# Weight chunks of experts 5 to 8 moved from the attention steps to between the routed jobs

## The reference

```
# attention: 4 sequences of 512 tokens, width 512; q and k come from ctx (width 128)
qp = ctx @ Wq.T + bq ;  kp = ctx @ Wk.T            (+ bk)
scores = qp @ kp.T * 128**-0.5 * layernorm(x)
x = x + softmax(where(mask, -inf, scores))
# feed-forward on xn = layernorm(x): one shared expert and the best 2 of 8
shared = silu(xn @ shared_gate_w) * (xn @ shared_up_w) @ shared_down_w
top_val, top_idx = top_k(xn @ router_w, 2) ;  p = sigmoid(top_val)
for each expert e: g, u = split((p_e * xn) @ gate_up_w[e]) ;  y_e = (silu(g) * u) @ down_w[e]
out = x + shared + sum of y_e over the two chosen experts
```

## Time and profile before

| | |
|---|---|
| median of 3 runs | 365.19 us (364.84 to 365.95) |
| the profiled execution | 365.61 us, its span 363.9 us |
| TensorE busy | 320.0 us (88%) |
| VectorE, ACT, GpSimd busy | 208.1, 177.6, 231.0 us |
| attention steps | from about 14 to 126 us |
| tables | about 126 to 162 us |
| routed jobs | about 162 us to the end |
| on ACT: exponential, and its sum read out | 0.73 and 0.19 us |
| two copies of x (L506, L507), two projections (L483) | 0.59 each; 1.25 the pair |
| high copy of a chunk (L493), copy of ctxT (L478), rw_hi (L538) | 1.04; 0.58; 0.23 us |
| idle of GpSimd before the scatters, for landings of earlier ones | 47.9 us in 21 waits |

### The profile page before, as it was taken

The page is one execution under the profiler, slowest core; times in us unless marked ns, Lnnn a source line. Parts: engine busy times, 40 slices in busy tenths (PEclk is TensorE's granted clock), DMA queues, the critical chain, the costliest instruction groups (busy, mean ns, idle before and its releaser), DMA issues.

```text
span 363.9 us, 6490 instructions
## 1 busy us (share of the span) xinstructions
PE 320.0 (88%) x1627; PEld 217.8 (60%) x1627; DVE 208.1 (57%) x461; ACT 177.6 (49%) x400; POOL 231.0 (63%) x199
## 2 busy tenths in 40 slices
PE   2857999899999994648999999999999999999991
PEld 1324666576666762315776766777777777777760
DVE  0666887898998889612444444444444444444440
ACT  2467767667757645102644434444444444444430
POOL 0688999886675739948376565656555465555433
PEclk9999999999999998556999999999999999999998
DMA  7956788746646420075346466857666666575736
GB/s 186 304 203 200 222 241 239 272 145 214 221 146 196 153 86 0 0 193 165 57 92 98 83 116 118 143 95 125 113 113 117 115 119 116 91 130 86 134 36 82
DMA packets 29763, 50.61 MB, mean 139 GB/s; under 512 B 5472, under 2 KB 9312, under 8 KB 29728
## 3 DMA queue, kind: packets, MB, share of 16 engines
q0 software_dynamic: 9008, 21.66, 33.7%
q1 hardware_dynamic: 19232, 27.99, 24.3%
q10 hardware_dynamic: 1488, 0.54, 0.7%
HBM read 30.45 MB, written 19.73 MB: 138 GB/s over the span
## 4 chain that ended last, share of the span: by engine, by line
PE 48%; POOL 19%; issue 10%; ACT 7%; DMA 7%; DVE 6%; POOLq 0%; SPq 0%; DVEq 0%; ACTq 0%
PE bank L948 9%; PE bank L958 8%; PE bank L953 8%; POOL gu_lo L356 7%; PE bank L981 5%; PE bank L987 5%; PE bank L984 5%; POOL dn_lo L356 5%; PE bank L1072 4%; DMA out_rows<-y,jscatter 3%; POOL rstd L332 3%; PE bank L967 2%; ACT gu_hi L493 2%; ACT bank L488 2%; POOL pen L351 2%
## 5 line engine op out<-in xcount | busy, mean ns | idle before, releaser
L439 POOL DMA_INDIRECT out_rows<-y,jscatter x39 | 61.9, 1588 | 73.5 <-DMA out_rows<-y,jscatter 47.9
L958 PE MATMUL bank<-gu_hi,x_lo 128*128 (+1 forms) x220 | 70.9, 444 | 0.0
L948 PE MATMUL bank<-gu_hi,x_hi 128*128 (+1 forms) x220 | 62.4, 406 | 3.4 <-POOL dn_lo L356 1.4
L953 PE MATMUL bank<-gu_lo,x_bf 128*128 (+1 forms) x220 | 57.5, 384 | 0.0
L670 DVE TENSOR_TENSOR x_lo<-bank,x_hi 128x512 fp32r<-128x512 f32 x55 | 37.7, 686 | 26.4 <-ACT x_bf L507 25.3
L863 DVE SCALAR_TENSOR_TENSOR h<-bank,xg,h 128x256 f32<-128x256 f32 x39 | 18.9, 484 | 58.4 <-ACT h L594 57.0
L420 POOL DMA_INDIRECT xg<-xn_rows,jgather x39 | 41.7, 1069 | 16.1 <-issue 15.1
L514 ACT CAST h_hi<-bank 128x256 fp32r<-128x256 f32 x55 | 20.6, 374 | 60.9 <-PE bank L967 59.0
L958 PEld LDWEIGHTS bank<-gu_hi,x_lo 128*128 128x128 f32 x220 | 42.0, 191 | 12.7 <-issue 0.3
L356 POOL TENSOR_TENSOR gu_lo<-stage,gu_hi 128x1024 bf16<-128x1024 f32 x18 | 43.4, 2412 | 9.7 <-ACT gu_hi L493 9.7
L948 PEld LDWEIGHTS bank<-gu_hi,x_hi 128*128 128x128 f32 x220 | 40.5, 190 | 13.7 <-issue 3.1
(11 more groups left out here) (128 smaller groups left out, 491.5 us busy)
## 6 DMA issues: line engine op xcount, KB each, us to landing
stage<-in_L_ffn_gate_up_w SPq DMA_DIRECT2D x16, 512.0 KB, 3.8
xin<-in_x SPq DMA_DIRECT2D x16, 256.0 KB, 4.3
xn_rows<-xn SPq DMA_DIRECT2D x16, 256.0 KB, 3.8
stage<-in_L_ffn_down_w SPq DMA_DIRECT2D x8, 512.0 KB, 3.8
out_rows<-x SPq DMA_DIRECT2D x16, 256.0 KB, 4.2
out_rows<-zeros POOLq DMA_DIRECT2D x1, 1024.0 KB, 5.0
ctx_in<-in_ctx SPq DMA_DIRECT2D x1, 768.0 KB, 8.8
xg<-xn_rows,jgather POOLq DMA_INDIRECT x39
```

Of the source, the lines that this page charges most:

```text
L439: g.indirect_dma_start(out=out, out_offset=bass.IndirectOffsetOnAxis(ap=jscatter[:, n - TILES:n - TILES + 1], axis=0), in_=y[:, r, :], in_ ...
L948: tn.matmul(ps_g(n)[:], x_hi[:, n % TS, k, :], gu_hi[:, e, k, :], start=(k == 0), stop=False)
L953: tn.matmul(ps_g(n)[:], x_bf[:, n % TS, k, :], gu_lo[:, e, k, :], start=False, stop=False)
L958: last = tn.matmul(ps_g(n)[:], x_lo[:, n % TS, k, :], gu_hi[:, e, k, :], start=False, stop=(k == KC - 1))
```

## The change

It lets `EARLY` be 15: each of the steps 3 to 14 converts one chunk, step 0 two, step 1 one, step 2 none. In the steps from 2 on the low part stands ahead of pair_inv_std, in the steps 0 and 1 behind it. Chunk 15 comes at the end of the attention, 16 to 18 behind the first gathers, and the other eight (19 to 26) in the jobs: their high copies in the jobs 2, 4, ... 16, their low parts behind the scatters of the jobs 3, 5, ... 17. CAREFUL becomes 20. In the first steps the order of projections, transposes, statistics and conversions is changed on all four engines, TensorE gets 8 + 14 transposes of the identity that nobody reads (keep_busy), and rw_hi and rw_lo move to step 1.

```diff
-EARLY = 3 * (E - 1)
+EARLY = 15
-CAREFUL = 8
+CAREFUL = 20
+SPREAD = CHUNKS - EARLY - 4
...
         def chunks(s):
-            return range(2 * s, 2 * s + 2) if s < 6 else range(s + 6, s + 7) if s < TILES - 1 else range(0)
+            if s == 0:
+                return range(0, 2)
+            return range(2, 3) if s == 1 else range(s, s + 1) if 3 <= s < TILES - 1 else range(0)
...  # GpSimd
             penalty(1)
-            first_inv_std(1)
             g.memset(zeros[:], 0.0).then_inc(zero_s, 1)
             pool.wait_ge(zero_s, 1)
             g.dma_start(out_t[TILES:TILES + XS].rearrange("r p d -> p r d"),
                         zeros[:].unsqueeze(1).to_broadcast([P, XS, D])).then_inc(st_trash, 16)
+            first_inv_std(1)
...
-                if i < 2:
+                if place >= 7 and i < 2:
...
-                else:
+                elif place >= 7:
                     pool.wait_ge(max_s, TILES)
                 low_part(c)
...
-                for c in chunks(s)[0:1]:
-                    low_part(c)
-                pair_inv_std(s)
-                for c in chunks(s)[1:]:
-                    low_part(c)
+                if s < LAG:
+                    pair_inv_std(s)
+                if s == 0:
+                    low_part(0)
+                elif s == 1:
+                    low_part(1)
+                    low_part(2)
+                else:
+                    for c in chunks(s):
+                        low_part(c)
+                    pair_inv_std(s)
...
                 scatter(n)
-                if n in (TILES + 1, TILES + 2):
-                    late_low(READY + 3 + n - TILES - 1)
+                if TILES + 3 <= n < TILES + 2 * SPREAD + 3 and (n - TILES) % 2:
+                    late_low(READY + 3 + (n - TILES - 3) // 2)
...  # ACT
             ctx_copy(1)
-            act.wait_ge(ld_rw, 16)
-            a.copy(rw_hi[:], rw[:]).then_inc(rwhi_s, 1)
...
                 expo(s)
-                if s + 1 < B:
-                    projections(s + 1)
-                if s + 2 < B:
-                    ctx_copy(s + 2)
+                if s == 0:
+                    projections(1)
+                    high_part(0)
+                    ctx_copy(2)
+                if s == 1:
+                    x_high(0)
+                    high_part(1)
+                    projections(2)
+                    high_part(2)
+                    ctx_copy(3)
+                    act.wait_ge(ld_rw, 16)
+                    a.copy(rw_hi[:], rw[:]).then_inc(rwhi_s, 1)
+                if s == 2:
+                    projections(3)
                 if j >= 0:
                     half_tanh(j)
-                for c in chunks(s):
-                    high_part(c)
-                if s >= 1:
+                if s >= 2:
+                    for c in chunks(s):
+                        high_part(c)
                     x_high(s - 1)
...
-                if n in (TILES + 1, TILES + 2):
-                    late_high(EARLY + 4 + n - TILES - 1)
+                if TILES + 2 <= n < TILES + 2 * SPREAD + 2 and (n - TILES) % 2 == 0:
+                    late_high(EARLY + 4 + (n - TILES - 2) // 2)
...  # VectorE
+            v.tensor_scalar(kpad_pen[:], kpad_in[:], MASKED, None, ALU.mult).then_inc(pen_ready, 1)
             x_stats(0)
             x_mean(0)
-            v.tensor_scalar(kpad_pen[:], kpad_in[:], MASKED, None, ALU.mult).then_inc(pen_ready, 1)
-            x_stats(1)
-            x_mean(1)
-            dve.wait_ge(rwhi_s, 1)
-            v.tensor_tensor(rw_lo[:], rw[:], rw_hi[:].bitcast(f32), ALU.subtract).then_inc(rwlo_s, 1)
             for s in range(TILES):
...
                 neg_max(s)
+                if s == 0:
+                    x_stats(1)
+                    x_mean(1)
...
                         x_low(s - 1)
+                    if s == 1:
+                        dve.wait_ge(rwhi_s, 1)
+                        v.tensor_tensor(rw_lo[:], rw[:], rw_hi[:].bitcast(f32), ALU.subtract).then_inc(rwlo_s, 1)
...  # TensorE
+            def keep_busy(count):
+                for _ in range(count):
+                    tn.transpose(bank[2][:, 0:P], ident[:], ident[:])
+
             pe.wait_ge(c_ident, 1)
+            keep_busy(8)
...
             last.then_inc(wT_ps, 1)
+            keep_busy(14)
             ctx_transpose(0)
             projections(0)
+            scores(0)
+            scores(1)
             ctx_transpose(1)
-            scores(0)
+            projections(1)
+            ctx_transpose(2)
...
-                if s + 1 < B:
-                    projections(s + 1)
-                if s + 2 < B:
-                    ctx_transpose(s + 2)
+                if s == 0:
+                    projections(2)
+                    ctx_transpose(3)
                 if j == 0:
+                    pe.wait_ge(lo_s, 2)
+                if j == 1:
                     pe.wait_ge(lo_s, 3)
...
-                if s + 1 < TILES:
+                if 1 <= s < TILES - 1:
                     scores(s + 1)
+                if s == 1:
+                    projections(3)
```

More of the change, by code:

```diff
@@ L536, in _ @@
             ctx_copy(1)
-            act.wait_ge(ld_rw, 16)
-            a.copy(rw_hi[:], rw[:]).then_inc(rwhi_s, 1)
             def late_high(c):
-                if c % 3 < 2:
+                if c >= 21 and c % 3 < 2:
                     act.wait_ge(score_ps, TILES)
-                else:
+                elif c >= 21:
                     act.wait_ge(pen_s, TILES)
```

## The result

The changed kernel takes 369.64 us (median of 4, 369.13 to 371.78) against 365.57 for the kernel before beside it: ratio 1.0126, interval 1.0100 to 1.0152. That is slower by some 4 to 5 us, and outside the forecast range of 361.8 to 368.8. The profiled execution took 369.98 us, its span is 368.2 us against 363.9.

What follows compares the result with a forecast made beforehand. GpSimd was taken to limit the early attention steps, TensorE the routed jobs. Terms -5.6 + 5.9 + 0.4 = +0.7 on 365.61 gave 366.3, put at 365.9 us against the median; 8-in-10 range 361.8 to 368.8.

Steps and rivals of the forecast that it cites:

- The steps with one chunk: Attention steps 3 to 6: one low part fewer per interval, each taking 6.73 us, a gain of 2.9 us.
- The warming transposes: Start: 22 dummy transposes on TensorE might end the first projections 1.8 us earlier; valued at nothing, 0 to 1 us lost.
- The first steps: Steps 0 to 2: reordered queues bring rstd(2) to 35.0 from 38.00, a gain of 3.0 us.
- a rival with 0.15: Step 1: TensorE's idling lowers its clock, rstd(2) comes 2 to 4 us later, time 368 to 369.5; chance 0.15.
- the late x(2): Step 0: x(2)'s load 1 us late, with step 1 another 1 us late, lowers the start-and-steps gain to 3.5 us.
- GpSimd among the jobs: Routed jobs: eight low parts delay GpSimd, S17 leaves at 265.3, TensorE waits for gathers; job 20 loses 5.9 us.
- What follows the wait at job 20: From job 20: everything behind moves by the same 5.9 us, jobs 4.75 us apart, no further lateness.
- The chunk loads beside the scatters: Routed jobs: loads of chunks 22 to 26 delay landings behind S4, S8, S12; 0.4 us taken, bounds 0 and 2.1.
- -5.6 + 5.9 + 0.4: Whole kernel: start-and-steps gain, loss up to job 20, and chunk-load delay in us, summing to +0.7.

Runs made afterwards that it cites:

- the fill: Changed kernel plus dummy identity transposes on idle TensorE: 22 ahead of projections(3) in step 1, 366.10 us; separately, 12 ahead of job 20's low-part wait, 367.82 us.

## Why the prediction was wrong, point by point

- **The steps with one chunk.** Right: intervals of 7.20, then 6.73; a gain of 2.4 from step 2 to step 14.
- **The warming transposes.** Right that they gain nothing: the early first scores end in the wait for x(2).
- **The first steps: the step that failed.** The prediction gave rstd(2) at 35.0, a gain of 3.0; it measured 0.6. The order of the work was read nearly rightly, since with TensorE kept busy rstd(2) starts at 35.23, or 17.95 us after x_stats(2); from the 17.15 that I counted with, that gives 35.1. What was wrong was to leave the clock at its full level in the sum. The idle stretch was there in the working (23.9 to 27.7; it was 24.6 to 28.4), the price too (3.75 us for projections(3); it took 3.61), but it stood as a rival with 0.15. The fill shows it as worth 1.5 of the 2.4 missing; 0.65 to 0.8 is the late x(2), which the bounds had. One more item was missed without harm: rw_lo was counted as before, at 0.19, and took 1.10, so that raw_scores(2) came later than 28.05 even with the fill (28.92).
- **GpSimd among the jobs.** Right: S17 was to come 52.9 us after S6 and came 53.2 after (208.77 to 261.95), TensorE waited for the gathers of jobs 8, 10 and 14, and job 20 lost 5.80 of the forecast 5.9. G18 didn't hold it up, G8 did. Single terms were off and made up for each other: S6 to S7 took 3.86 and not 3.27, S8 to S9 and S12 to S13 took 0.1 and 0.2 less.
- **What follows the wait at job 20: the second miss.** The prediction said that everything behind it moves by as much. In the profiled execution TensorE's own pause cost another 1.7 us through the clock, which the step priced as nothing. The experiments with CAREFUL 27 and with the fill remove it together with the wait and by itself (3.9 and 2.4 us by the medians). That the fall comes with some of these waits and not with all (one of three profiles) stays unexplained. I had looked for the clock's fall in an idle stretch of 4 us and not behind one of 1.8.
- **The chunk loads beside the scatters.** The 0.4 was for nothing: from the scatters S4, S8 and S12, whose landings the chain waits for, to the next ones it took 5.87, 5.97 and 5.76 against 5.76, 6.09 and 6.00 before. The reason that I gave for the small value, that a scatter's own data start late in its landing, no run shows. The rule of the Trainium skill (DMA: Bandwidth & Descriptors, "Queues, rings and completion order"), that a DMA engine takes packets from its queue rows in turn, speaks for a sharing; the trace shows none that sets a time here.
- **The sum.** -5.6 + 5.9 + 0.4 became -3.1 + 5.8 + 1.7 - 0.1 = +4.3. The range of 361.8 to 368.8 left out that the clock can fall twice. Two falls are worth 3.2 of the 3.6 us between +0.7 and +4.3; the late x(2) adds some 0.7 to them, and the 0.4 for nothing goes off.

The Trainium skill (TensorE: Matmul & The Clock Gate, "Why this matters for your kernels") warns of idle gaps between bursts of matmuls. The trace agrees for the 3.84 us of step 1, but the length of the gap alone doesn't decide. At job 20 the clock fell behind an idle row of 1.82 us in one profile and not behind 1.90 or 1.29 in two others. In step 1 it had fallen already behind 2.21 and 2.38 us in two profiles (CAREFUL 27, and the low parts spread further), and the 3.20 us of the old order were followed by either level.

Open is why executions of one kernel differ by 2 to 4 us (the changed kernel with the old first steps took 368.33 to 372.49). The profiles show falls of the clock at different jobs, but there is one profile for each kernel only (two for the kernel before).

## What to carry to other kernels

Before work is moved to an engine "with idle time", list its waits one by one: a 2.3 us operation costs little behind an operation whose successor must wait for a landing, and can cost its full length one place further on. A wait for "everything" (here the first job that isn't in CAREFUL) turns a late helper into a stop of the engine that bounds the kernel, though nothing that this job needs is late. And where a change lets TensorE idle in a new place, price its clock into the sum: some 1.5 to 1.8 us for most of the falls here, and a few transposes into a free bank can avoid them. Price it as a risk and not as a certainty: the same gap was followed by a fall in one execution and not in another.

## What the runs showed of the hardware

- The granted clock fell to 0.50 within 2 us behind an idle of only 1.82 us on TensorE at job 20 of the changed kernel. It didn't fall with 12 transposes in that stretch, and neither without them in two other profiles with idle rows of 1.90 and 1.29 us there.
- The move of rw_lo to step 1 lets it meet a low part on GpSimd, and this VectorE operation on 128 x 32 elements took 1.10 us; in the kernel before, with no low part beside it, 0.19 (0.16 in the second profile). It took 1.01 to 1.11 in the seven other profiles of the new order, and 0.97 with the old first steps and the new chunks (at 14.04, beside an operation of GpSimd that ran from 13.82 to 14.96). In all nine GpSimd's operation had begun first and rw_lo ended 0.04 to 0.06 us behind its end (in the changed kernel 29.64 behind 29.60), so rw_lo's length is the rest of GpSimd's operation. Beside rstd, an operation of GpSimd on 128 x 1 elements (12.96 to 13.54 in the kernel before), it was not held up. The Trainium skill (GPSIMD Engine Reference, "Specifications") states that the two engines share their SBUF interfaces, and names VectorE instructions with two SBUF inputs, which this one is. A VectorE operation with one of its inputs in a bank of PSUM shows nothing of the kind: x_lo took 0.69 at 29.23 in the kernel before, with a low part on GpSimd from 27.36 to 29.71, and 0.66 at 25.64 in the changed one, with none beside it.
